# Last three down products in two PSUM banks, the last remainder on DVE, and the last output store in four

## The chip, the cores and the metric

The kernel runs on one core of one Trainium2 chip. The metric is the device time of one execution in microseconds (us); a lower number is better. The engines are PE (TensorE, matrix products, with PEld for its weight loads), DVE (VectorE), ACT (ScalarE), POOL (GpSimd) and SP (SyncE, which here only issues DMA transfers). PE writes into PSUM, which has eight banks of 128 x 512 fp32; DVE and ACT read PSUM, POOL doesn't.

## The reference

`x` is 4 sequences x 512 tokens x 128 features. Four residual layers follow each other: a gated state-space layer, a mixture of experts, a time-mixing layer (RWKV), and the same mixture of experts again. Only the last one's end is touched by the change. It is:

```python
x = hidden_states.reshape(-1, h)
scores = jax.nn.softmax(x @ gate_w, axis=-1)
topk_w, topk_idx = jax.lax.top_k(scores, K)
topk_w = topk_w / (jnp.sum(topk_w, axis=-1, keepdims=True) + 1e-20)
onehot = jax.nn.one_hot(topk_idx, E, dtype=x.dtype)
w_per_expert = jnp.einsum('nke,nk->ne', onehot, topk_w)
for e in range(E):
    hid = jax.nn.silu(x @ w_gate[e]) * (x @ w_up[e])
    y = y + w_per_expert[:, e:e + 1] * (hid @ w_down[e])
shared = jax.nn.silu(x @ ws_gate) * (x @ ws_up) @ ws_down
return (y + shared).reshape(b, s, h)
```

with 8 experts, 2 chosen for each token, and a hidden width of 256; its input is the layer-normed `x`, and its result is added to `x`. All is in fp32; the kernel splits each fp32 operand of these products into an fp16 high part and an fp16 remainder and makes three products of them.

## The kernel before

The last three layers run in one phase, `phase_body`. Each engine has its own stream of instructions, written out by hand; between engines only semaphores order the work (`wait_ge` and `then_inc`).

The experts' work is cut into 8 slots (`q`), four sequences for the first mixture and four for the second, and each slot into 9 branches (`e`; 0 is the shared one). A unit `u = 9 q + e` is one branch on one sequence of 512 tokens, and there are UNITS = 72. The time-mixing layer of each sequence is laid in between (`beside`), the last of it well before the last slot. In a unit:

- `gate_up(u, blk)` on PE makes the gate and the up product for each half `blk` of the hidden width, 3 matmuls each (L1571, L1572, L1575), in banks 0 to 3.
- `gate` on ACT (L1762) applies silu; `hidden` on DVE (L1925) multiplies by the up product into `hid`.
- `high` on ACT (L1769) casts `hid` to fp16, `hid_hi`; `low` on POOL (L2160) makes the remainder `hid_lo = hid - hid_hi` and increments `lo_ready`.
- `down(u)` on PE makes for each of the four 128-token tiles 6 matmuls (L1590 to L1592), 24 in all, into one bank, `down_ps` (bank 4), and increments `down_made`. It waits for `lo_ready` 2(u + 1) and for `added` u, since the add of the unit before reads the same bank.
- `add(u)` on DVE (L1941) adds the four tiles, each with its tokens' expert weights, from `down_ps` into `x`; the last of the four increments `added`.

PE's stream is gate_up(u), then down(u - 2); after gate_up(71) come down(69), down(70) and down(71) with nothing between. DVE's is add(u - 3), then the two `hidden` of u; at its end stand add(69), add(70) and add(71). POOL's ends with the three remainders (70, 1), (71, 0), (71, 1). Bank 5, `ps_t`, serves for turning (transposing) tiles and for parts of the time-mixing layer; its last use is the turn of slot 7's input, read by ACT, which then increments `normT_ready` to 7.

SP stores a sequence of the output when `added` says that its ninth branch is in: one transfer of 256 KB per sequence (L2315), 128 partitions x 4 tiles x 512 bytes. Its last instruction waits for all stores.

Of the kernel before, what the change touches and what calls it, by code (L numbers as in the profile page):

```python
# [13 lines left out]
P = 128  # L14
SEQS, SEQ = 4, 512
TPS = SEQ // P
# [11 lines left out]
FBLK = FFN // P  # L28
# [9 lines left out]
ALU = mybir.AluOpType  # L38
# [1391 lines left out]
def of_seq(s):  # L1430

    return slice(TPS * s, TPS * (s + 1))
# [9 lines left out]
def phase_body(core, io, lns, moe_x):  # L1442
# [4 lines left out]
    nc = core.nc  # L1447
    SLOTS = 2 * SEQS
    UNITS = SLOTS * BRANCHES
    HB = HIDDEN // P  # L1450
    with ExitStack() as ctx:
        def sb(name, shape, dt=F32):
            return ctx.enter_context(nc.sbuf_tensor("b_" + name, shape, dt))

        def sem(name):
            return core.semaphore("b_" + name)

        x, w = core.x, core.wsplit
# [7 lines left out]
        hid = sb("hid", [P, 4, SEQ])  # L1466
        hid_hi = sb("hid_hi", [P, 3 * FBLK, SEQ], F16)
        hid_lo = sb("hid_lo", [P, 3 * FBLK, SEQ], F16)
# [42 lines left out]
        gate_ps, up_ps, down_ps = core.banks[0:2], core.banks[2:4], core.banks[4]  # L1511
        ps_t, ps_k, ps_v = core.banks[5:8]

        def table(k):
# [5 lines left out]
        recip = ps_k  # L1522

        gate_made, up_made, down_made = core.gate_made, core.up_made, sem("down")
        silu_ready, hid_ready, hi_ready, lo_ready, added = sem("silu"), sem("hid"), sem("hid_hi"), sem("hid_lo"), sem("added")
        veps_in, rstd_in, normed, x_turned, normT_ready, x_hi_ready, x_lo_ready = (
            sem("veps_in"), sem("rstd_in"), sem("normed"), sem("x_turned"), sem("normT"), sem("x_hi"), sem("x_lo"))
# [17 lines left out]
        dve_step, pool_step, act_step, stored = sem("dve_step"), sem("pool_step"), sem("act_step"), sem("stored")  # L1545
# [14 lines left out]
        def _(pe):  # L1560
# [15 lines left out]

            def down(u):
                e = u % BRANCHES
                pe.wait_ge(lo_ready, 2 * (u + 1))
                if u:  # L1580
                    pe.wait_ge(added, u)
                for c in range(TPS):
                    dst = down_ps[:, P * c:P * (c + 1)]
                    for blk in range(FBLK):
                        slot = FBLK * (u % 3) + blk
                        h_hi = hid_hi[:, slot, P * c:P * (c + 1)]
                        h_lo = hid_lo[:, slot, P * c:P * (c + 1)]
                        d_hi = w[:, e, 4, P * blk:P * (blk + 1)]
                        d_lo = w[:, e, 5, P * blk:P * (blk + 1)]
                        nc.tensor.matmul(dst, h_hi, d_hi, start=blk == 0, stop=False)  # L1590
                        nc.tensor.matmul(dst, h_hi, d_lo, start=False, stop=False)  # L1591
                        ins = nc.tensor.matmul(dst, h_lo, d_hi, start=False, stop=blk == FBLK - 1)  # L1592
                ins.then_inc(down_made, 1)
# [151 lines left out]
            for u in range(UNITS + 2):  # L1745
                if u < UNITS:
                    if u:
                        gate_up(u, 0)
                    beside(u, 0)
                    if u:  # L1750
                        gate_up(u, 1)
                    beside(u, 1)
                if u >= 2:
                    down(u - 2)
                if u < UNITS:
                    beside(u, 2)
# [155 lines left out]
        def _(dve):  # L1912
# [7 lines left out]
            def hidden(u, blk):  # L1920
                dve.wait_ge(silu_ready, 2 * u + blk + 1)
                dve.wait_ge(up_made, 2 * u + blk + 1)
                if u >= 2:
                    dve.wait_ge(lo_ready, 2 * (u - 2) + blk + 1)
                nc.vector.scalar_tensor_tensor(hid[:, 2 * (u % 2) + blk, :], up_ps[blk][:, :], GU_UNSCALE * H_SCALE,  # L1925
                                               silu[:, 2 * (u % 2) + blk, :], ALU.mult, ALU.mult).then_inc(hid_ready, 1)

            def add(u):
                q, e = divmod(u, BRANCHES)
                s = q % SEQS  # L1930
                dve.wait_ge(down_made, u + 1)
                if e == 0:
                    nc.vector.scalar_tensor_tensor(x[:, of_seq(s), :], down_ps[:, :]
                                                   .rearrange("p (c d) -> p c d", c=TPS), DOWN_UNSCALE,
                                                   x[:, of_seq(s), :], ALU.mult, ALU.add).then_inc(added, 1)
                    return
                if e == 1:
                    dve.wait_ge(routed, q + 1)
                for c in range(TPS):
                    i = TPS * s + c  # L1940
                    ins = nc.vector.scalar_tensor_tensor(x[:, i, :], down_ps[:, P * c:P * (c + 1)],  # L1941
                                                         w_branch[:, q % 2, e, c:c + 1], x[:, i, :], ALU.mult, ALU.add)
                ins.then_inc(added, 1)

            def all_experts(ap):
# [190 lines left out]
                        aggregate(ln_m2, s, veps_in)  # L2136

            for u in range(UNITS + 3):
                if u >= 3:
                    add(u - 3)  # L2140
                if u < UNITS:
                    beside(u, 0)
                    hidden(u, 0)
                    beside(u, 1)
                    hidden(u, 1)
                    beside(u, 2)

        @block.gpsimd
        def _(pool):
# [7 lines left out]
            def low(u, blk):  # L2157
                pool.wait_ge(hi_ready, 2 * u + blk + 1)
                slot = FBLK * (u % 3) + blk
                nc.gpsimd.tensor_tensor(hid_lo[:, slot, :], hid[:, 2 * (u % 2) + blk, :], hid_hi[:, slot, :],  # L2160
                                        ALU.subtract).then_inc(lo_ready, 1)
# [136 lines left out]
            for u in range(UNITS):  # L2298
# [3 lines left out]
                beside(u, 1)  # L2302
                low(u, 0)
                beside(u, 2)
            low(UNITS - 1, 1)

        @block.sync
        def _(sp):
            core.clear_retired(sp)
            for dst, name in ((w_rkvo, "w_rkvo"), (w_fk, "w_fk"), (w_fr, "w_fr"), (w_fv, "w_fv")):  # L2310
                sp.dma_start(dst[:], io[name]).then_inc(w_b_in, 16)
            dst = io["out"].rearrange("s (c p) d -> s p c d", p=P)
            for s in range(SEQS):
                sp.wait_ge(added, (SEQS + s + 1) * BRANCHES)
                sp.dma_start(dst[s], x[:, of_seq(s), :]).then_inc(stored, 16)  # L2315
            sp.wait_ge(stored, 16 * SEQS)


class Shared:
# [3 lines left out]
def program(nc, io, stop_after=9):  # L2323
    core = Core(nc)
    with ExitStack() as top:
        constants(core, top)
        ln_moe1, ln_moe2, ln_tm, ln_cm = (LayerNorm(nc, top, name) for name in ("ln_moe1", "ln_moe2", "ln_tm", "ln_cm"))
        moe_x = (top.enter_context(nc.sbuf_tensor("normT_moe", [P, SEQ], F32)),
                 top.enter_context(nc.sbuf_tensor("x_hi", [P, 2, SEQ], F16)),
                 top.enter_context(nc.sbuf_tensor("x_lo", [P, 2, SEQ], F16)))  # L2330
        with ExitStack() as mamba:
            sh = Shared()
            sh.normT, sh.x_hi, sh.x_lo = moe_x

            def sb(name, shape, dt=F32):
                return mamba.enter_context(nc.sbuf_tensor(name, shape, dt))
            sh.ln = ln_moe1
            sh.norm = sb("norm", [P, TILES, P])
            sh.q = sb("q", [P, TILES, P])
            sh.xbc = sb("xbc", [P, CONV_BLOCKS, TOKENS])  # L2340
            sh.sz = sb("sz", [P, TILES, INNER])
            sh.xtok = sb("xtok", [P, TILES, XTOK])
            sh.moe_raw = sb("moe_raw", [P, MOE_RING, 3 * FFN])
            sh.w_out = sb("w_out", [P, 2, P])
            sh.w_out_in = top.enter_context(nc.semaphore("w_out_in"))
            phase_mamba(core, io, sh)
            core.end_phase()
        phase_body(core, io, (ln_moe1, ln_moe2, ln_tm, ln_cm), moe_x)
        core.end_phase()
        core.end_phase()  # L2350
# [63 lines left out]
```

## Time and profile before

| | |
|---|---|
| median of 3 runs | 497.91 us (497.86 to 498.1) |
| the profiled execution | 496.6 us |
| span of its trace, first to last instruction | 494.9 us |
| PE busy | 470.8 us (95%) |
| DVE busy | 389.5 us (79%) |
| ACT busy | 355.9 us (72%) |
| POOL busy | 366.7 us (74%) |
| first product of down(69) | 483.85 us |

The profile is of one execution. Busy time is what the engine's own instructions cover; issuing a DMA, waiting and branching aren't counted. A row in order of time gives the start, the duration, the engine, the line, the tile written and the tiles read, how many instructions were merged (x4), and in brackets how long the engine had been idle and which instruction released it. PE's matmuls are pipelined: a row of 0.22 us may start 0.06 us behind the one before. The span leaves out what lies around the program; the median of the runs is 1.3 us above the profiled execution.

### The profile page before, as it was taken

To read this page: it belongs to the slowest core of one execution; us is meant where nothing else is said; L and a number is where in the kernel's file an instruction comes from. 1 tells how busy PE (TensorE), PEld (TensorE's weight loads), DVE (VectorE), ACT (ScalarE), POOL (GpSimd) and SP (SyncE) were. 2 spreads that over 40 slices of the span, in tenths; PEclk is the share of its full clock that TensorE was granted. 3 is DMA by queue.
4 is the path that set the end of the run, shared out by engine and by line. 5 is a ranking of instruction groups with operands and counts; after the bars stand their busy time and mean duration, and the time that the engine had idled before them with its cause. 6 is when DMAs were issued, how large, how long until landed. Compare 5 with 4: busy or idle time off the path is not lost.

```text
span 494.9 us, 10643 instructions
## 1 busy us (share of the span) xinstructions
PE 470.8 (95%) x3706; PEld 325.5 (66%) x3706; DVE 389.5 (79%) x1043; ACT 355.9 (72%) x687; POOL 366.7 (74%) x449
## 2 busy tenths in 40 slices
PE   7898999999899999999999999999999989999994
PEld 7575789988466666656566756576566766766663
DVE  5899999677767878799888897889887868487663
ACT  1699999774857767964996759695868576858551
POOL 4755896986485775899878978987989585366652
PEclk9999999999999999999999999999999999999999
DMA  8000212000200000000000000000000000000000
GB/s 270 20 2 11 66 53 66 1 1 3 71 1 1 1 1 2 3 0 1 2 1 1 3 1 1 1 1 2 2 23 1 1 1 23 2 2 1 21 1 23
DMA packets 7013, 8.51 MB, mean 17 GB/s; under 512 B 560, under 2 KB 5168, under 8 KB 6960
## 3 DMA queue, kind: packets, MB, share of 16 engines
q1 hardware_dynamic: 6960, 7.83, 4.9%
q8 instruction: 30, 0.49, 0.4%
q14 instruction: 23, 0.19, 0.1%
HBM read 6.78 MB, written 1.05 MB: 16 GB/s over the span
## 4 chain that ended last, share of the span: by engine, by line
PE 55%; DVE 9%; POOL 5%; ACT 3%; issue 2%; DVEq 0%; POOLq 0%; ACTq 0%
PE bank L1571 9%; PE bank L1575 9%; PE bank L1572 9%; PE bank L1590 5%; PE bank L1592 5%; PE bank L1591 5%; PE bank L1707 3%; PE bank L1690 2%; PE bank L1633 2%; DVE x L1941 2%; PE bank L1634 2%; POOL b_hc L2222 1%; PE bank L1597 1%; DVE b_hid L1925 1%; PE bank L1618 1%
## 5 line engine op out<-in xcount | busy, mean ns | idle before, releaser
L2160 POOL TENSOR_TENSOR b_hid_lo<-b_hid,b_hid_hi 128x512 f16<-128x512 f32 x144 | 168.0, 1179 | 51.4 <-ACT b_hid_hi L1769 49.3
L1925 DVE SCALAR_TENSOR_TENSOR b_hid<-bank,b_silu 128x512 f32<-128x512 f32 x144 | 97.7, 688 | 55.4 <-ACT b_silu L1762 38.1
L1762 ACT ACTIVATE b_silu<-bank 128x512 f32<-128x512 f32 x144 | 85.9, 597 | 57.6 <-PE bank L1575 56.5
L1571 PE MATMUL bank<-x_hi,wsplit 128*128 128x512 f16 x284 | 107.7, 379 | 2.4 <-ACT b_silu L1762 1.9
L1575 PE MATMUL bank<-x_lo,wsplit 128*128 128x512 f16 x284 | 107.6, 379 | 0.0
L1572 PE MATMUL bank<-x_hi,wsplit 128*128 128x512 f16 x284 | 107.6, 379 | 0.0
L1590 PE MATMUL bank<-wsplit,b_hid_hi 128*128 128x128 f16 x576 | 100.2, 219 | 4.3 <-DVE x L1941 2.6
L1769 ACT CAST b_hid_hi<-b_hid 128x512 f16<-128x512 f32 x144 | 88.2, 612 | 22.2 <-DVE b_hid L1925 22.0
L1592 PE MATMUL bank<-wsplit,b_hid_lo 128*128 128x128 f16 x576 | 100.2, 219 | 0.0
L1591 PE MATMUL bank<-wsplit,b_hid_hi 128*128 128x128 f16 x576 | 100.2, 219 | 0.0
L1941 DVE SCALAR_TENSOR_TENSOR x<-bank,b_w_branch,x 128x128 f32<-128x128 f32 x256 | 71.5, 342 | 15.5 <-PE bank L1592 15.4
L1590 PEld LDWEIGHTS bank<-wsplit,b_hid_hi 128*128 128x128 f16 x576 | 56.6, 98 | 15.2 <-POOL b_hid_lo L2160 5.6
L1591 PEld LDWEIGHTS bank<-wsplit,b_hid_hi 128*128 128x128 f16 x576 | 56.3, 98 | 7.1 <-issue 1.3
L1592 PEld LDWEIGHTS bank<-wsplit,b_hid_lo 128*128 128x128 f16 x576 | 56.3, 98 | 0.0
L1575 PEld LDWEIGHTS bank<-x_lo,wsplit 128*128 128x128 f16 x284 | 27.8, 98 | 33.6
L1571 PEld LDWEIGHTS bank<-x_hi,wsplit 128*128 128x128 f16 x284 | 27.9, 98 | 29.7 <-issue 2.9
L1572 PEld LDWEIGHTS bank<-x_hi,wsplit 128*128 128x128 f16 x284 | 27.8, 98 | 26.7 <-issue 4.0
L520 DVE SCALAR_TENSOR_TENSOR xbc<-bank,cols,xbc 128x511 f32<-128x511 f32 (+2 forms) x48 | 35.6, 746 | 1.8 <-ACT xbc L783 0.7
L1114 PE MATMUL bank<-causal,seg_l 128*128 128x128 f32 x128 | 17.2, 278 | 0.4 <-ACT expo L828 0.2
L1145 PEld LDWEIGHTS bank<-xdt,mix 128*128 128x128 f32 x128 | 16.4, 192 | 0.7
L1114 PEld LDWEIGHTS bank<-causal,seg_l 128*128 128x128 f32 x128 | 15.9, 192 | 1.4 <-issue 0.9
L341 POOL TENSOR_TENSOR g<-y,sz 128x256 f32<-128x256 f32 x16 | 13.2, 825 | 4.5 <-DVE y L595 4.5
(246 smaller groups left out, 946.4 us busy)
## 6 DMA issues: line engine op xcount, KB each, us to landing
moe_raw<-in_moe SPq DMA_DIRECT2D x9, 384.0 KB, 4.1
x<-in_x SPq DMA_DIRECT2D x4, 256.0 KB, 3.9
out<-x SPq DMA_DIRECT2D x4, 256.0 KB, 2.3
rope<-in_rope SPq DMA_DIRECT2D x1, 512.0 KB, 6.2
wzx<-in_wzx SPq DMA_DIRECT2D x1, 386.0 KB, 6.5
b_w_rkvo<-in_w_rkvo SPq DMA_DIRECT2D x1, 256.0 KB, 2.7
b_w_fk<-in_w_fk SPq DMA_DIRECT2D x1, 256.0 KB, 2.9
b_w_fv<-in_w_fv SPq DMA_DIRECT2D x1, 256.0 KB, 3.4
```

The source lines that it names most:

```text
L520: ins = nc.vector.scalar_tensor_tensor(xbc[:, b, t0 + back:t1], conv_ps[b % 2][:, 0:SEQ - back], col(core, "conv_w", TAPS * b + TAPS - 1 - ...
L1571: nc.tensor.matmul(dst, hi, x_hi[:, q % 2, :], start=True, stop=False)
L1572: nc.tensor.matmul(dst, lo, x_hi[:, q % 2, :], start=False, stop=False)
L1575: nc.tensor.matmul(dst, hi, x_lo[:, q % 2, :], start=False, stop=True).then_inc(made, 1)
L1590: nc.tensor.matmul(dst, h_hi, d_hi, start=blk == 0, stop=False)
L1591: nc.tensor.matmul(dst, h_hi, d_lo, start=False, stop=False)
L1592: ins = nc.tensor.matmul(dst, h_lo, d_hi, start=False, stop=blk == FBLK - 1)
L1762: nc.scalar.activation(silu[:, 2 * (u % 2) + blk, :], gate_ps[blk][:, :], ACT.Silu, scale=GU_UNSCALE).then_inc(silu_ready, 1)
L1769: nc.scalar.copy(hid_hi[:, FBLK * (u % 3) + blk, :], hid[:, 2 * (u % 2) + blk, :]).then_inc(hi_ready, 1)
L1925: nc.vector.scalar_tensor_tensor(hid[:, 2 * (u % 2) + blk, :], up_ps[blk][:, :], GU_UNSCALE * H_SCALE, silu[:, 2 * (u % 2) + blk, :], ALU. ...
L1941: ins = nc.vector.scalar_tensor_tensor(x[:, i, :], down_ps[:, P * c:P * (c + 1)], w_branch[:, q % 2, e, c:c + 1], x[:, i, :], ALU.mult, AL ...
L2160: nc.gpsimd.tensor_tensor(hid_lo[:, slot, :], hid[:, 2 * (u % 2) + blk, :], hid_hi[:, slot, :], ALU.subtract).then_inc(lo_ready, 1)
```

## The change

Three edits, all at the end of the program. The down products of units 69 and 71 go to bank 5 and the one of 70 stays in bank 4; the waits follow, so that a down product waits for the reader of its own bank. The remainder (71, 1) is made by DVE (`last_low`, with a semaphore of its own), ahead of add(69) in DVE's stream, and no longer by POOL. The last sequence is stored in four transfers of 64 KB, one for each 128-token tile, each released by that tile's add.

```diff
+        def down_bank(u):
+
+            return ps_t if u in (UNITS - 3, UNITS - 1) else down_ps
...
+        last_lo = sem("last_lo")
...
             def down(u):
                 e = u % BRANCHES
-                pe.wait_ge(lo_ready, 2 * (u + 1))
-                if u:
+                if u == UNITS - 1:
+                    pe.wait_ge(lo_ready, 2 * UNITS - 1)
+                    pe.wait_ge(last_lo, 1)
+                else:
+                    pe.wait_ge(lo_ready, 2 * (u + 1))
+                if u == UNITS - 3:
+                    pe.wait_ge(normT_ready, SLOTS - 1)
+                if u > UNITS - 3:
+                    pe.wait_ge(added, u - 1)
+                elif u and u < UNITS - 3:
                     pe.wait_ge(added, u)
                 for c in range(TPS):
-                    dst = down_ps[:, P * c:P * (c + 1)]
+                    dst = down_bank(u)[:, P * c:P * (c + 1)]
...
+            def last_low():
+
+                u = UNITS - 1
+                slot = FBLK * (u % 3) + FBLK - 1
+                dve.wait_ge(hi_ready, 2 * UNITS)
+                nc.vector.tensor_tensor(hid_lo[:, slot, :], hid[:, 2 * (u % 2) + FBLK - 1, :], hid_hi[:, slot, :],
+                                        ALU.subtract).then_inc(last_lo, 1)
+
             def add(u):
...
                 dve.wait_ge(down_made, u + 1)
+                if u > UNITS - 3:
+                    dve.wait_ge(added, u)
...
                 for c in range(TPS):
                     i = TPS * s + c
-                    ins = nc.vector.scalar_tensor_tensor(x[:, i, :], down_ps[:, P * c:P * (c + 1)],
+                    ins = nc.vector.scalar_tensor_tensor(x[:, i, :], down_bank(u)[:, P * c:P * (c + 1)],
                                                          w_branch[:, q % 2, e, c:c + 1], x[:, i, :], ALU.mult, ALU.add)
+                    if u == UNITS - 1 and c < TPS - 1:
+                        ins.then_inc(added, 1)
                 ins.then_inc(added, 1)
...
             for u in range(UNITS + 3):
+                if u == UNITS:
+                    last_low()
                 if u >= 3:
                     add(u - 3)
...
-            low(UNITS - 1, 1)
...
-            for s in range(SEQS):
+            for s in range(SEQS - 1):
                 sp.wait_ge(added, (SEQS + s + 1) * BRANCHES)
                 sp.dma_start(dst[s], x[:, of_seq(s), :]).then_inc(stored, 16)
-            sp.wait_ge(stored, 16 * SEQS)
+            for c in range(TPS):
+                sp.wait_ge(added, UNITS + c)
+                sp.dma_start(dst[SEQS - 1][:, c, :], x[:, TPS * (SEQS - 1) + c, :]).then_inc(stored, 16)
+            sp.wait_ge(stored, 16 * (SEQS - 1 + TPS))
```

The end of DVE's stream before, from the `hidden` pair of unit 71 on; the rows of L1941 are the adds of units 68 to 71, and the square brackets name what a row waits for:

```order
L1941 SCALAR_TENSOR_TENSOR x<-bank4,b_w_branch,x 128x128 x3
L1925 SCALAR_TENSOR_TENSOR b_hid<-bank2,b_silu 128x512 [waits b_hid_lo,up_made,b_silu]
L1925 SCALAR_TENSOR_TENSOR b_hid<-bank3,b_silu 128x512 [waits b_hid_lo,up_made,b_silu]
L1941 SCALAR_TENSOR_TENSOR x<-bank4,b_w_branch,x 128x128 [waits b_down]
L1941 SCALAR_TENSOR_TENSOR x<-bank4,b_w_branch,x 128x128 x3
L1941 SCALAR_TENSOR_TENSOR x<-bank4,b_w_branch,x 128x128 [waits b_down]
L1941 SCALAR_TENSOR_TENSOR x<-bank4,b_w_branch,x 128x128 x3
```

The same place now (L1939 is `hidden`, L1965 the add):

```order
L1965 SCALAR_TENSOR_TENSOR x<-bank4,b_w_branch,x 128x128 x3
L1939 SCALAR_TENSOR_TENSOR b_hid<-bank2,b_silu 128x512 [waits b_hid_lo,up_made,b_silu]
L1939 SCALAR_TENSOR_TENSOR b_hid<-bank3,b_silu 128x512 [waits b_hid_lo,up_made,b_silu]
L1947 TENSOR_TENSOR b_hid_lo<-b_hid,b_hid_hi 128x512 [waits b_hid_hi]
L1965 SCALAR_TENSOR_TENSOR x<-bank5,b_w_branch,x 128x128 [waits b_down]
L1965 SCALAR_TENSOR_TENSOR x<-bank5,b_w_branch,x 128x128 x3
L1965 SCALAR_TENSOR_TENSOR x<-bank4,b_w_branch,x 128x128 [waits b_added,b_down]
L1965 SCALAR_TENSOR_TENSOR x<-bank4,b_w_branch,x 128x128 x3
```

The remainder has moved in ahead of add(69), add(69) and add(71) read bank 5, and add(70) and add(71) wait for `added` as well. The last add of each list, like the one above it, is left out.

The end of SP's stream before, from the weight loads at the phase's start on:

```order
L2311 DMA b_w_rkvo<-in_w_rkvo 128x512
L2311 DMA b_w_fk<-in_w_fk 128x512
L2311 DMA b_w_fr<-in_w_fr 128x128
L2311 DMA b_w_fv<-in_w_fv 128x512
L2315 DMA out<-x 128x4x128 [waits b_added] x4
L1451 UNCONDITIONAL_BRANCH [waits b_stored]
```

And now:

```order
L2338 DMA b_w_rkvo<-in_w_rkvo 128x512
L2338 DMA b_w_fk<-in_w_fk 128x512
L2338 DMA b_w_fr<-in_w_fr 128x128
L2338 DMA b_w_fv<-in_w_fv 128x512
L2342 DMA out<-x 128x4x128 [waits b_added] x3
L2345 DMA out<-x 128x128 [waits b_added] x4
L1451 UNCONDITIONAL_BRANCH [waits b_stored]
```

One store of four tiles has become four stores of one tile.

## Rows read from the trace of the kernel before

**Rows 1.** The page, engines: busy us, share of the span, instructions

```profile
PE 470.8 (95%) x3706; PEld 325.5 (66%) x3706; DVE 389.5 (79%) x1043; ACT 355.9 (72%) x687; POOL 366.7 (74%) x449
```

**Rows 2.** DVE in order of time, the tail (start us, duration us)

```profile
481.46 1.12 DVE L1941 SCALAR_TENSOR_TENSOR x<-bank,b_w_branch,x 128x128 f32<-128x128 f32 x4 [0.58 <-PE bank L1592]
482.82 0.69 DVE L1925 SCALAR_TENSOR_TENSOR b_hid<-bank,b_silu 128x512 f32<-128x512 f32 x1 [0.23 <-ACT b_silu L1762]
...
485.39 1.13 DVE L1941 SCALAR_TENSOR_TENSOR x<-bank,b_w_branch,x 128x128 f32<-128x128 f32 x4 [0.58 <-PE bank L1592]
488.21 1.13 DVE L1941 SCALAR_TENSOR_TENSOR x<-bank,b_w_branch,x 128x128 f32<-128x128 f32 x4 [1.69 <-PE bank L1592]
491.02 1.13 DVE L1941 SCALAR_TENSOR_TENSOR x<-bank,b_w_branch,x 128x128 f32<-128x128 f32 x4 [1.68 <-PE bank L1592]
```

**Rows 3.** PE in order of time: down(69)'s last product, first of 70 and 71

```profile
485.14 0.22 PE L1592 MATMUL bank<-wsplit,b_hid_lo 128*128 128x128 f16 x1
486.67 0.22 PE L1590 MATMUL bank<-wsplit,b_hid_hi 128*128 128x128 f16 x1 [1.31 <-DVE x L1941]
...
489.48 0.22 PE L1590 MATMUL bank<-wsplit,b_hid_hi 128*128 128x128 f16 x1 [1.31 <-DVE x L1941]
```

**Rows 4.** Chain that ended last, 480 to 496 us (start, us, what)

```profile
490.99 0.03 issue
491.02 0.35 DVE x L1941
```

**Rows 5.** ACT and POOL in order of time, the tail

```profile
482.11 0.60 ACT L1762 ACTIVATE b_silu<-bank 128x512 f32<-128x512 f32 x1 [1.53 <-PE bank L1575]
...
484.90 0.62 ACT L1769 CAST b_hid_hi<-b_hid 128x512 f16<-128x512 f32 x1 [0.39 <-DVE b_hid L1925]
484.59 2.27 POOL L2160 TENSOR_TENSOR b_hid_lo<-b_hid,b_hid_hi 128x512 f16<-128x512 f32 x2
```

**Rows 6.** DVE groups: busy us, mean ns | idle before; L2071: min/median/max ns

```profile
L626 DVE TENSOR_TENSOR x_lo<-normT_moe,x_hi 128x512 f16<-128x512 f32 x1 | 0.7, 684 | 0.0
L1962 DVE TENSOR_TENSOR b_shift<-bank,b_best 128x32 f32<-128x32 f32 x8 | 1.5, 192 | 0.3
L2071 DVE SCALAR_TENSOR_TENSOR b_mixed<-b_dif,cols,b_hcT x8: 741/1698/1753, 259.6 to 416.7; 128x512 f32<-128x512 f32 x8
```

**Rows 7.** DVE and POOL in order of time, around 112 us

```profile
112.20 0.68 DVE L626 TENSOR_TENSOR x_lo<-normT_moe,x_hi 128x512 f16<-128x512 f32 x1
111.69 0.62 POOL L314 TENSOR_TENSOR dx<-xtok,cols 128x256 f32<-128x256 f32 x1
```

**Rows 8.** SP's DMA issues in order of time (start us, us on SP)

```profile
6.64 2.13 SPq L245 DMA_DIRECT2D moe_raw<-in_moe  x3
...
130.26 0.33 SPq L2311 DMA_DIRECT2D b_w_rkvo<-in_w_rkvo  x1
130.64 0.51 SPq L2311 DMA_DIRECT2D b_w_fk<-in_w_fk  x1
131.20 0.42 SPq L2311 DMA_DIRECT2D b_w_fr<-in_w_fr  x1
131.67 0.43 SPq L2311 DMA_DIRECT2D b_w_fv<-in_w_fv  x1
...
492.17 0.37 SPq L2315 DMA_DIRECT2D out<-x  x1
```

**Rows 9.** DMA: us to landing; tenths busy, 129:137; stages: engines' busy, clock, share, GB/s

```profile
out<-x SPq DMA_DIRECT2D x4, 256.0 KB, 2.3
b_w_fr<-in_w_fr SPq DMA_DIRECT2D x1, 64.0 KB, 3.0
...
DMA  0000000100044979979978778435000000000000
...
493.00:493.10 0.10, 0.00 (x0) 0.00 (x0) 0.00 (x0) 0.00 (x0) 0.00 (x0) 1.00 0.09 26
494.00:494.10 0.10, 0.00 (x0) 0.00 (x0) 0.00 (x0) 0.00 (x0) 0.00 (x0) 1.00 0.26 67
```

More of the change, by code:

```diff
@@ L1931, in add @@
                 dve.wait_ge(down_made, u + 1)
+                if u > UNITS - 3:
+                    dve.wait_ge(added, u)
                 if e == 0:
-                    nc.vector.scalar_tensor_tensor(x[:, of_seq(s), :], down_ps[:, :]
+                    nc.vector.scalar_tensor_tensor(x[:, of_seq(s), :], down_bank(u)[:, :]
                                                    .rearrange("p (c d) -> p c d", c=TPS), DOWN_UNSCALE,
```

## The prediction

> **What bounds the kernel now.** Read first the engines' shares, then the last 11 us of DVE and PE in order of time with what released each, then the chain in the same stretch. Over the whole span PE is busy 95% [rows 1]; the change leaves everything up to unit 69 alone, so only the tail is of interest. There the picture differs from the rest: DVE's last two adds stood idle 1.69 and 1.68 us for PE [rows 2], and PE's first products of units 70 and 71 stood idle 1.31 us each for DVE's add [rows 3]. Each waits for the other, because the down product of a unit and its add share one bank. In the order of time [rows 2, 3]: down(69) issues its last product at 485.14, add(69) runs 485.39 to 486.52, down(70) runs from 486.67, add(70) 488.21 to 489.34, down(71) from 489.48, add(71) 491.02 to 492.15. So a round is 2.81 us: 1.13 of add, about 0.15 to release PE, 1.51 of 24 products, 0.03 to release DVE [rows 2 to 4]. Steady units don't show this: there gate and up products of a later unit stand between two down products. After add(71) comes the store: SP issues at 492.17, data moves from about 493.05 to 494.05, the store has landed 2.3 us after its issue, at 494.47, and the span ends at 494.9, another 0.43 [rows 8, 9]. The profiled execution took 496.6 us for a span of 494.9; the median of the runs is 497.91, 1.3 above. All that changes is in a tail that both contain once, so I subtract microseconds from either alike.
>
> **Two banks.** down(69) goes to bank 5, whose last reader (normT_ready 7, the scaling of slot 7's turned input) stands seven units earlier in the code, so that wait costs nothing; it starts where it starts now, since its predecessor's add, done at 482.58 [rows 2], didn't hold it. down(70) uses bank 4 and needs only added 69, met at 482.58, and the remainder of (70, 1), which POOL had made before it began the next at 484.59 [rows 5]. It follows directly: the 24 products of a unit stand 0.056 apart (from 486.67 the last ends 1.51 later, itself 0.22 long [rows 3, 4]), so it starts at 485.20, its 24 take 1.35 to issue, its end is about 486.72 instead of 488.18. The first of the two stalls of 1.31 is gone. down(71) goes to bank 5 and must wait for add(69), which reads it. With nothing else changed add(69) ends at 486.52, and PE's turn would be at 486.72; next late would be POOL's remainder of (71, 1), whose last two operations end at 484.59 + 2.27 = 486.86 [rows 5]. So what remains of the second stall is set by the third edit.
>
> **The last remainder on DVE.** It replaces a POOL operation (half of those 2.27, ending at 486.86) by a DVE TENSOR_TENSOR of the same form, 128x512 f32 to f16, two SBUF inputs. The trace of before has exactly one such on DVE, L626, 0.684 us [rows 6]. It waits for ACT's last cast, 484.90 + 0.62 = 485.52, plus the 0.11 that DVE took after an ACT activation (482.11 + 0.60 to 482.82) [rows 2, 5]: it starts at 485.63 and ends at 486.31. But it stands ahead of add(69) on DVE, and add(69) could have started at 485.39. The queued work behind it is add(69), (70) and (71), and PE's down(71) waits for the first. add(69) becomes 486.32 to 487.45. That delays its end by 0.93, while the remainder itself is done 0.55 earlier than on POOL: on this path the move costs more than it gives, against the other two edits alone (PE at about 486.95). down(71): 487.45 + 0.15 = 487.60, + 1.51 = 489.11, + 0.03: add(71) starts at **489.14 instead of 491.02, 1.88 us earlier**. add(70), with its new wait for added 70, takes 487.50 to 488.63 (a wait between dependent DVE operations is 0.04: L1962, 0.3 us idle in 8 [rows 6]), half a microsecond before add(71) is released: hidden. The lower bound of the DVE start is 0.08 less, since DVE operations without a wait between them overlap by that much (the first of the four adds takes 0.35, all four 1.13 [rows 2, 4]).
>
> Is DVE slowed by sharing memory access with POOL? DVE's L2071, also with two SBUF inputs, takes 741 ns at best and 1698 at the median [rows 6]; the long ones may be ones that meet POOL. The POOL operation on (71, 0), the first of those 2.27 us, ends at about 485.73, 0.1 us after DVE's would start. L626 gives the case that fits: it began at 112.20 under a POOL operation that ran until 112.31, and took 0.684 [rows 6, 7]. I add nothing, and keep up to 0.96 (1698 - 741) as a rival. The Trainium skill, GPSIMD Engine Reference, in its table of properties, says that POOL's memory interface is shared with VectorE and contends with instructions that have two SBUF inputs. By that alone the operation could be the slow kind and 1.88 would shrink to about 0.9; the row of L626 says that an overlap this short is free.
>
> **Four transfers.** Before, from the start of add(71) to the end: 1.13 + 0.02, then 2.3, then 0.43, in all 3.88. Now tile 0 is released after its own 0.35 [rows 4], SP starts at 489.14 + 0.35 + 0.02 = 489.51. Tiles 1 to 3 are ready at 0.26 us each, but SP issues more slowly: the four weight loads start at 130.26, 130.64, 131.20 and 131.67, a pitch of 0.47; they range from 0.38 to 0.56 [rows 8]. So the last issue is at 489.51 + 3 x 0.47 = 490.92, which is 0.63 later than a single transfer's (490.29). SP's issue takes the place of DVE as the last wait. What a lone store of 64 KB needs the trace doesn't show. Built from the 256 KB store: 0.88 until data moves, 1.0 of data, 0.42 until landed [rows 9]; a quarter of the data is 0.25, so 1.55. Bounds: 1.55 and the full 2.3. I take 1.55, for the four weight loads, last issued at 131.67, moved data without a pause from the 12th to the 28th fifth of a microsecond behind 129, thus from 131.2 to 134.6 [rows 9], so neighbours overlap. End: 490.92 + 1.55 + 0.43 = 492.90; from the start of add(71) that is 3.76 against 3.88, a gain of 0.12 only. The sum is **1.88 + 0.12 = 2.00 us**: span 492.9, median 497.91 - 2.00 = **495.9**. The same pieces with a pitch of 0.38 give 2.27, with 0.56 give 1.73; with 0.71, the pitch of the three L245 that stood behind nine queued transfers [rows 8], 1.28. The DVE overlap can add 0.08 to each.
>
> The Trainium skill, DMA: Bandwidth & Descriptors, section "Anatomy of one DMA — SWDGE (gpsimd) path", puts a DMA at about 2.0 us fixed plus bytes over 436 GB/s and says that most of the fixed part is the write receipt: it speaks against splitting. Estimated from that page, 64 KB would need 2.15 where I count 1.55, and the total gain would be 1.4; for the 256 KB store it gives 2.6 where this trace has 2.3. It is weighed as the first rival.
>
> **Rivals.** (1) Landing doesn't shrink with size: a 64 KB store needs the same 2.3 as 256 KB. Then the tail after add(71) is 0.37 + 1.41 + 2.3 + 0.43 = 4.51, 0.63 worse than before, and the gain is 1.25: 496.7. For it: the 64 KB weight load took 3.0 [rows 9]. Against it: that one was queued behind 512 KB, and the store's own rows show a microsecond of data in the 2.3. The page named above would come near this. (2) DVE's remainder is held by POOL and costs 0.96 more: gain 1.0, 496.9. It needs POOL's (71, 0) to hold DVE's whole operation for an overlap of 0.1. (3) Slower: the queue works the four stores off one after another, each to its receipt. Each then holds it for 1.55: 489.51 + 4 x 1.55 + 0.43 = 496.14, 1.2 over 494.9: 499.1. The kernel is slower from 1.24 us a store on. Against it stands the row of the four loads, which carried data without a gap. (4) The change does not do what it says, because DVE is now the wait: add(69) still stands before down(71). That I have counted in; it is why the gain is 1.9 and not the 2.6 of both stalls. A larger gain, 2.35 and more, needs a quick SP and a landing below 1.55.
>
> **How the numbers follow.** Forecast, 495.6 to 496.3: 64%. (1) 496.7: 15%. (2) 496.9: 9%, two thirds of it within 0.2% of before. (3) 499.1: 4%. Larger gain, below 495.6: 8%. The likeliest is 495.9. From 495.4 to 496.8 the range leaves out (3), most of (2) and the outer end of the larger gain, with (1) and what lies between taken in: near 2 in 10 with what I can't foresee. 0.2%, about what a measurement can tell from no change, is 1.0 us: faster is below 496.9, thus 64 + 15 + 8 + 3 = 90%, same 6%, slower 4%.
>
> **What would show it.** Right: PE's first product of down(70) stands 0.06 behind the last of down(69), with no idle; one PE stall of about 0.9 us is left, ahead of down(71), released by DVE's add; DVE shows the remainder of about 0.68 before add(69), and add(69) starts near 486.3; add(71) starts 1.9 earlier; four SP issues at a pitch near 0.47, the last 0.6 after DVE's last add; landing of each about 1.5. Wrong: a DVE remainder of 1.2 or more (2), landings of 2.3 (1), landings that grow from first to fourth by over a microsecond each (3), or any shift before 483.85, which nothing here accounts for.

## The result, and the profile after

| | before | after |
|---|---|---|
| median | 497.28 us (16 runs, 495.71 to 498.10) | 495.05 us (16 runs, 494.49 to 496.12) |
| profiled execution, its span | 496.6, 494.9 us | 494.99, 493.3 us |
| down(69)'s first product to the span's end ("tail") | 11.05 us | 8.95 us |

The ratio is 0.9959 with a 95% interval of 0.995 to 0.9969: faster by 2.0 us (1.5 to 2.5). The forecast gain was 2.00. The absolute time, 495.05, lies below the low end of 495.4. More runs of the kernel before stood beside these; over all 16 its median is 497.28, not the 497.91 of the three runs that the prediction started from. A span is given to 0.1 us, so a tail is known to about 0.05.

DVE's tail after, in order of time, which answers to [rows 2]:

```profile
484.61 0.69 DVE L1939 SCALAR_TENSOR_TENSOR b_hid<-bank,b_silu 128x512 f32<-128x512 f32 x1 [0.60 <-PE bank L1581]
486.04 0.75 DVE L1947 TENSOR_TENSOR b_hid_lo<-b_hid,b_hid_hi 128x512 f16<-128x512 f32 x1 [0.74 <-ACT b_hid_hi L1783]
486.71 2.34 DVE L1965 SCALAR_TENSOR_TENSOR x<-bank,b_w_branch,x 128x128 f32<-128x128 f32 x8
489.51 1.13 DVE L1965 SCALAR_TENSOR_TENSOR x<-bank,b_w_branch,x 128x128 f32<-128x128 f32 x4 [0.46 <-PE bank L1606]
```

PE's, which answers to [rows 3]: the first product of unit 69, the two rows around the border between 69 and 70 (485.63, 485.69), and the last of 70 and the first of 71:

```profile
484.35 0.22 PE L1604 MATMUL bank<-wsplit,b_hid_hi 128*128 128x128 f16 x1
...
485.63 0.22 PE L1606 MATMUL bank<-wsplit,b_hid_lo 128*128 128x128 f16 x1
485.69 0.22 PE L1604 MATMUL bank<-wsplit,b_hid_hi 128*128 128x128 f16 x1
...
486.97 0.22 PE L1606 MATMUL bank<-wsplit,b_hid_lo 128*128 128x128 f16 x1
487.98 0.22 PE L1604 MATMUL bank<-wsplit,b_hid_hi 128*128 128x128 f16 x1 [0.79 <-DVE x L1965]
```

Both stalls of 1.31 us are no more; one of 0.79 is left, and DVE's add releases it. ACT's last cast runs 485.39 to 486.01, so DVE's remainder begins 0.03 behind it. SP's stores, and their time to landing, which answer to [rows 8, 9]:

```profile
489.89 1.77 SPq L2345 DMA_DIRECT2D out<-x  x4
```

```profile
out<-x SPq DMA_DIRECT2D x4, 64.0 KB, 1.6
```

Four issues take 1.77 us; DVE has been done since 490.64 when the last one begins at about 491.23.

Everything below is counted from the first product of down(69), so that what happens earlier drops out.

| from down(69)'s first product, us | before | forecast | after |
|---|---|---|---|
| DVE's remainder starts | none | 1.78 | 1.69 |
| add(69) starts | 1.54 | 2.47 | 2.36 |
| down(71) starts | 5.63 | 3.75 | 3.63 |
| add(71) starts | 7.17 | 5.29 | 5.16 |
| span ends | 11.05 | 9.05 | 8.95 |

### The profile page after: what moved, and what is told of

It reads as the page before. It is cut to its first block, busy times and chain, and to the rows that moved or that the text cites. A ratio compares the mean times of both kernels' runs of the same rounds, so it can differ in the third digit from the quotient of the medians.

```text
span 493.3 us, 10648 instructions
## 1 busy us (share of the span) xinstructions
PE 471.2 (96%) x3706; PEld 326.2 (66%) x3706; DVE 390.1 (79%) x1044; ACT 355.8 (72%) x687; POOL 365.6 (74%) x448
## 4 chain that ended last, share of the span: by engine, by line
PE 54%; DVE 9%; POOL 5%; ACT 4%; issue 2%; DVEq 0%; ACTq 0%; POOLq 0%
PE bank L1577 9%; PE bank L1581 9%; PE bank L1578 9%; PE bank L1604 5%; PE bank L1606 5%; PE bank L1605 5%; PE bank L1721 3%; PE bank L1704 2%; PE bank L1647 2%; PE bank L1648 2%; POOL b_hc L2250 1%; DVE x L1965 1%; DVE b_hid L1939 1%; PE bank L1611 1%; PE bank L1632 1%
## 5 line engine op out<-in xcount | busy, mean ns | idle before, releaser
L1939 DVE SCALAR_TENSOR_TENSOR b_hid<-bank,b_silu 128x512 f32<-128x512 f32 x144 | 97.7, 688 | 55.4 <-ACT b_silu L1776 38.1
L1965 DVE SCALAR_TENSOR_TENSOR x<-bank,b_w_branch,x 128x128 f32<-128x128 f32 x256 | 71.5, 341 | 12.1 <-PE bank L1606 11.9
```

What stands on the lines that cost most here:

```text
L1965: ins = nc.vector.scalar_tensor_tensor(x[:, i, :], down_bank(u)[:, P * c:P * (c + 1)], w_branch[:, q % 2, e, c:c + 1], x[:, i, :], ALU.mul ...
```

## The experiments

### Which edit carries what

Three kernels take one or two of the edits, from the changed kernel. Two banks alone:

```diff
             def down(u):
-                if u == UNITS - 1:
-                    pe.wait_ge(lo_ready, 2 * UNITS - 1)
-                    pe.wait_ge(last_lo, 1)
-                else:
-                    pe.wait_ge(lo_ready, 2 * (u + 1))
+                pe.wait_ge(lo_ready, 2 * (u + 1))
...
-                if u == UNITS:
-                    last_low()
...
+            low(UNITS - 1, 1)
```

and one store of the last sequence as in the kernel before. Where the remainder isn't ahead of it, add(69) also waits for `added` 69, which has long been reached.

> Two banks alone; the last remainder on POOL as before and one store of 256 KB. Theory A: from the first product of down(69), add(69) starts at 1.54 us, down(71) waits for POOL's last remainder (3.01, plus some 0.1) and add(71) starts at 4.64 instead of 7.17 before and 5.16 in the changed kernel; the tail is 8.5 us against 11.05 and 8.95; some 2.5 us faster than before. Rival B (moving the remainder to DVE is what lets the banks pay): add(71) starts at 5.2 or later and the tail is 9.0 or more.

> Two banks and four stores, the last remainder on POOL: the changed kernel without its edit on DVE. Theory A: tail 8.4 us, 0.5 shorter than the changed kernel's 8.95, some 2.6 us faster than before. Rival B: tail 8.95 or more.

> Two banks and the remainder on DVE, one store of 256 KB: the changed kernel without its four stores. Theory A: add(71) starts 5.16 after the first product of down(69) as in the changed kernel, 3.88 follow, tail 9.04: 2.0 us faster than before and 0.1 slower than the changed kernel. Rival (four stores carry a good part of the gain): tail 9.4 or more.

Measured, from the profiles:

| kernel | add(69) | down(71) | add(71) | add(71) to end | tail | ratio to before (95%) |
|---|---|---|---|---|---|---|
| before | 1.54 | 5.63 | 7.17 | 3.88 | 11.05 | 1 |
| all three edits | 2.36 | 3.63 | 5.16 | 3.79 | 8.95 | 0.9959 (0.995 to 0.9969) |
| banks | 1.54 | 3.06 | 4.61 | 3.86 | 8.47 | 0.9951 (0.9935 to 0.9966) |
| banks, four stores | 1.54 | 3.06 | 4.61 | 3.76 | 8.37 | 0.9945 (0.9928 to 0.9961) |
| banks, remainder on DVE | 2.36 | 3.62 | 5.15 | 3.82 | 8.97 | 0.9955 (0.9937 to 0.9974) |

Banks with four stores, PE and then POOL in order of time:

```profile
486.89 0.23 PE L1600 MATMUL bank<-wsplit,b_hid_hi 128*128 128x128 f16 x1 [0.22 <-POOL b_hid_lo L2182]
```

```profile
483.26 3.57 POOL L2182 TENSOR_TENSOR b_hid_lo<-b_hid,b_hid_hi 128x512 f16<-128x512 f32 x3 [1.48 <-ACT b_hid_hi L1779]
```

POOL ends at 486.83 and PE stands idle only 0.22. Each tail came out within 0.1 us of what theory A gave: the banks bring 2.6, the four stores 0.1 at most (8.47 to 8.37 with POOL's remainder, 8.97 to 8.95 with DVE's), and making the remainder on DVE takes back 0.5 to 0.6. The ratios of the three variants lie within 0.001 of each other and their intervals overlap, so this ranking rests on the profiles, whose tails carry little of the scatter described below: the kernel before, profiled twice, has 11.05 and 11.00.

The two smaller edits alone, on one bank:

> The kernel before with only the last remainder moved to DVE, ahead of add(69); one bank, one store. Theory A: add(69) starts 2.36 us after the first product of down(69) instead of 1.54, everything behind it shifts by this, tail 11.05 + 0.82 = 11.87: 0.8 us slower than before. Rival: the move costs nothing, because PE's down(71) no longer waits for POOL: tail 11.05 or less.

> The kernel before with only its last store split in four. Theory A: from the start of add(71) to the end 3.79 us instead of 3.88, tail 10.95; no difference that a median can tell. Rival (the landing of a small store is what counts): landings of 64 KB take 2.3, tail 11.7.

```profile
487.14 1.11 DVE L1961 SCALAR_TENSOR_TENSOR x<-bank,b_w_branch,x 128x128 f32<-128x128 f32 x4
489.93 1.13 DVE L1961 SCALAR_TENSOR_TENSOR x<-bank,b_w_branch,x 128x128 f32<-128x128 f32 x4 [1.68 <-PE bank L1602]
492.75 1.13 DVE L1961 SCALAR_TENSOR_TENSOR x<-bank,b_w_branch,x 128x128 f32<-128x128 f32 x4 [1.68 <-PE bank L1602]
```

These are the three adds with only the remainder moved (first product of down(69) at 484.78): add(69) starts at 2.36, the round of 2.8 us stays, the tail is 11.82, and the kernel is slower: 498.50 us, ratio 1.0027 (1.0015 to 1.0039). Without the banks the edit on DVE is a loss by itself. The tail shows 0.77 of it, near the 0.8 expected; the 1.3 of the ratio is more than the edit costs, because all ten runs of this kernel have the drop of the clock described below, and nine of the 19 runs beside them. Against those nine (median 498.06) it is 0.44 slower. Only the last store split: tail 10.93, ratio 0.9998 (0.9986 to 1.0011), no difference. Both tails are as theory A had them.

### Where the remainder stands, and whether POOL holds DVE

> The changed kernel with DVE's remainder behind add(69) instead of ahead of it. Theory A: add(69) at 1.54 to 2.67 from the first product of down(69), the remainder until 3.35, down(71) released by it at 3.5, add(71) at 5.0, tail 8.8, 0.15 shorter than the changed kernel. Rival (the order on DVE makes no difference): tail 8.95.

```diff
-                if u == UNITS:
-                    last_low()
                 if u >= 3:
                     add(u - 3)
+                if u == UNITS:
+                    last_low()
```

Its add(69) waits for `added` 69 too. Tail 8.66 against 8.95, better than the 8.8 expected: DVE starts the remainder at 2.58, before add(69) ends at 2.67, it takes 0.68, and PE starts down(71) at 3.36, released by it. So the order within DVE matters, 0.3 us here. The ratio is 0.9934 (0.991 to 0.996); with four runs it can't be told from the changed kernel's.

> The changed kernel, and POOL makes the last remainder a second time, into a tile that nobody reads, released by the same cast as DVE's. So both engines run an operation with two SBUF inputs side by side. If POOL holds DVE (the second rival of the prediction, made to happen): DVE's remainder takes 1.4 to 1.8 us instead of 0.75 and the tail grows from 8.95 by as much. If the two only share and lose little: 0.75 to 0.85, tail 9.0.

```diff
+            pool.wait_ge(hi_ready, 2 * UNITS)
+            nc.gpsimd.tensor_tensor(lo_twice[:], hid[:, 2 * ((UNITS - 1) % 2) + FBLK - 1, :], hid_hi[:, slot, :],
+                                    ALU.subtract)
```

DVE, then POOL:

```profile
484.52 0.75 DVE L1948 TENSOR_TENSOR b_hid_lo<-b_hid,b_hid_hi 128x512 f16<-128x512 f32 x1 [0.74 <-ACT b_hid_hi L1784]
```

```profile
484.68 1.60 POOL L2336 TENSOR_TENSOR b_lo_twice<-b_hid,b_hid_hi 128x512 f16<-128x512 f32 x1
```

DVE's operation has POOL's beside it for all but its first 0.16 us and takes the same 0.75; POOL's takes 1.60 instead of 1.16 (the median of its 143 others). The tail is 8.88. Here DVE began first, and POOL was the one that lost. It is one pair in one profile.

The other order stands in the trace before, at the long L2071 [rows 6] that the prediction's second rival was priced from. DVE and POOL:

```profile
259.60 1.70 DVE L2071 SCALAR_TENSOR_TENSOR b_mixed<-b_dif,cols,b_hcT 128x512 f32<-128x512 f32 x1
415.27 2.13 DVE L2071 SCALAR_TENSOR_TENSOR b_mixed<-b_dif,cols,b_hcT 128x512 f32<-128x512 f32 x2
```

```profile
259.58 1.17 POOL L2160 TENSOR_TENSOR b_hid_lo<-b_hid,b_hid_hi 128x512 f16<-128x512 f32 x1
413.80 2.39 POOL L2160 TENSOR_TENSOR b_hid_lo<-b_hid,b_hid_hi 128x512 f16<-128x512 f32 x2
```

At 259.60 POOL began 0.02 ahead, kept its 1.17, and DVE took 1.70. The last two L2071 start at 415.27 and 416.67; POOL is done at 416.19, and the first takes 1.47, the second, with POOL idle, 0.74. The six of 1.69 to 1.75 all stand beside POOL operations with two inputs. So the rival's mechanism exists, at the price of up to 0.96 that it was given, where POOL began first and the two overlapped for long. In the changed kernel POOL also began first, but the overlap was 0.20 us (POOL until 486.24, DVE from 486.04), and the remainder took 0.75; in the kernel with the remainder behind add(69), with POOL done, it took 0.68, so at most 0.07 went to it. No run starts a long overlap in POOL's favour on purpose.

### The stores

> Two banks, the last remainder on POOL, and the last sequence stored in two transfers of 128 KB (tiles 0 and 1, tiles 2 and 3) instead of four. Theory A (SP's pitch of some 0.47 us bounds four stores, 0.6 us behind DVE's last add): with two, the last issue follows DVE's last add at once, 1.15 after the start of add(71); landing 0.88 + 0.5 + 0.42 = 1.8; with the last 0.43, 3.4 us from the start of add(71) instead of 3.76 to 3.79 with four and 3.88 with one; tail 8.0 against 8.37. Rival (what counts is the size of the last transfer): tail 8.4 or more.

```diff
-            for c in range(TPS):
-                sp.wait_ge(added, UNITS + c)
+            for a, b in [(0, 2), (2, 4)]:
+                sp.wait_ge(added, UNITS + b - 1)
```

DVE's last adds, SP's issues, and the issues with KB and us to landing:

```profile
489.48 1.13 DVE L1961 SCALAR_TENSOR_TENSOR x<-bank,b_w_branch,x 128x128 f32<-128x128 f32 x4 [0.61 <-PE bank L1602]
```

```profile
490.12 0.89 SPq L2340 DMA_DIRECT2D out<-x  x2
```

```profile
out<-x SPq DMA_DIRECT2D x2, 128.0 KB, 1.8
```

From the start of add(71) to the end 3.42 us, forecast 3.4; with four stores 3.76 to 3.79, with one 3.82 to 3.88. Two stores gain what four give away to SP's pitch. This too rests on the profiles: the ratio, 0.9932 (0.9916 to 0.9949), overlaps the 0.9945 (0.9928 to 0.9961) of two banks with four stores. The stores land 2.3, 1.8 and 1.6 us after issue for 256, 128 and 64 KB.

### Why the absolute time missed

The kernel before, unchanged, under another label:

> The kernel before, unchanged. Theory A (the gain was right and the absolute time missed only because three runs of the kernel before stood at the upper end of its scatter): its median is within 0.2% of the kernel before that runs beside it, its runs scatter over about 2 us, and where they differ, the difference is there before the first router product of the last phase, not in the tail. Rival B (the changed kernel gained more than the tail holds, through something earlier): the kernel before scatters by less than 1 us, and its tail, 11.05 us from the first product of down(69) to the span's end, differs from run to run.

Its median is 496.81 us (11 runs, 496.38 to 498.05), ratio 0.9997 (0.9987 to 1.0007). The scatter of 1.7 us is there with nothing changed, and its profiled tail is 11.00, as before. Where the scatter is made shows in the start-up loop: PE multiplies an identity 22 times (44 matmuls, L1183) while the first tokens are normalised. Its row before, with two banks alone, and with banks and remainder on DVE:

```profile
2.27 7.42 PE L1183 MATMUL bank<-ident 128*128 128x128 f32 x44 [2.27 <-POOL after L265]
```

```profile
2.27 8.06 PE L1183 MATMUL bank<-ident 128*128 128x128 f32 x44 [2.27 <-POOL after L265]
```

```profile
2.26 6.54 PE L1183 MATMUL bank<-ident 128*128 128x128 f32 x44 [2.26 <-POOL after L265]
```

The same loop takes 6.54 to 8.06 us in the profiles, and the first router product of the last phase starts at 126.2, 126.9 and 125.3: in all twelve profiles with this loop the start is the loop's duration plus 118.7 to 118.9. The changed kernel's profile has 7.92 and 126.8, the one before 7.42 and 126.2, which is the 0.5 us by which its down(69) starts later (484.35, 483.85). In the loop a matmul takes about 0.18 us at first and 0.09 later, and the switch comes between 3 and 6 us behind the loop's start. By stages of 2 us (the first bracket counts PE's matmuls), banks and remainder on DVE:

```profile
4.00:6.00 2.00, 2.00 (x15) 2.00 (x15) 1.13 (x9) 0.00 (x0) 0.73 (x1) 1.00 0.91 263
6.00:8.00 2.00, 2.00 (x21) 2.00 (x20) 1.93 (x12) 0.00 (x0) 1.14 (x4) 1.00 1.02 321
```

and two banks alone:

```profile
4.00:6.00 2.00, 2.00 (x11) 2.00 (x11) 1.03 (x8) 0.00 (x0) 0.82 (x1) 1.00 0.92 269
6.00:8.00 2.00, 2.00 (x12) 2.00 (x11) 1.85 (x12) 0.00 (x0) 0.95 (x4) 1.00 0.99 320
```

Between 6 and 8 us the one makes 21 and the other 12. The granted clock reads 1.00 (2.4 GHz) in all of these rows, so what makes them slow isn't seen in it.

There is a second source. In four profiles (remainder alone, split alone, two stores, tile banks) PE's granted clock drops between 130 and 140 us. Remainder alone, by stage:

```profile
125.00:130.00 5.00, 3.90 (x22) 1.99 (x20) 3.25 (x13) 4.10 (x7) 1.95 (x16) 1.00 0.01 2
130.00:135.00 5.00, 3.85 (x11) 1.39 (x12) 3.56 (x13) 4.04 (x8) 3.32 (x3) 0.71 0.53 174
135.00:140.00 5.00, 5.00 (x47) 3.16 (x46) 2.31 (x4) 2.71 (x6) 4.32 (x9) 0.95 0.00 0
```

Behind the engines' columns stands the granted clock: 0.71 of 2.4 GHz as a mean over five microseconds, a mixture of the levels 2.4 and 1.2 GHz; by single microseconds it reads 0.56, 0.50, 0.50 and 0.73 from 132 to 136. PE had been busy 3.90 of the 5 us ahead of it; in the kernel before, profiled without a drop, it was 4.54, but the kernel with 16 start-up products (below) had 3.63 and no drop, so what sets it off stays open. From the first router product to down(69) these four take 359.2 to 359.3 us, the ten profiles without a drop 357.4 to 357.6. The loop with 1.5 us and the drop with 1.7 cover the range of 2.4 us that the kernel before has.

Whether a run had the drop can be read without its profile, from the mean granted clock of the whole run: it is 0.995 or 0.997 for these four and 0.998 or more for the other ten. It is on record for 54 more runs of the kernel before, the 11 above and 43 beside the experiments:

| mean granted clock | before: runs, us, median | changed kernel: runs, us, median |
|---|---|---|
| 0.999 to 1.000 | 31, 495.56 to 497.27, 496.75 | 12, 494.49 to 495.15, 494.89 |
| 0.995 to 0.997 | 23, 497.37 to 498.18, 497.86 | 4, 495.48 to 496.12, 495.83 |

The two groups don't overlap. The three runs of the prediction, 497.86 to 498.10, lie where only runs with a drop lie (their own clocks aren't on record), and the profiled execution, 496.6 with a clock of 1.000, in the other group. Like against like the change gains 1.9 and 2.0 us by these medians, though the runs didn't stand side by side.

> The changed kernel with 16 instead of 22 products in the start-up loop that keeps PE busy until the first tokens are normalised. Ten profiles say that the first router product of the last phase starts 118.8 us after that loop's duration, which varies from 6.54 to 8.06 us. Theory A (the scatter of absolute times, and so the base of the prediction, comes from this loop, which ends later than its tokens): the loop takes 5.9 us or less, the first router product starts at 125.0 or earlier, and the median falls by some 0.8 us below the changed kernel's 495.05. Rival (PE's clock is what rises late, and the products behind the loop only run slow in its place): the start stays between 125.3 and 126.9.

```diff
-            warm_up(22)
+            warm_up(16)
```

Its PE in order of time:

```profile
2.27 5.89 PE L1183 MATMUL bank<-ident 128*128 128x128 f32 x32 [2.27 <-POOL after L265]
7.99 1.08 PE L1018 MATMUL bank<-ident,norm 128*128 128x128 f32 x4
```

The loop takes 5.89 as expected and the first router product starts at 125.2, not 125.0 or before. The first four real products take 1.08 us where they take 0.60 in the kernel before, but the slow stretch didn't move into them: PE makes 12 matmuls between 7 and 8 us, as many as anywhere in the loop. They wait for the tokens. DVE normalises the first four tiles here, 0.26 us apart and the last until 8.69, and PE's four products start 0.25 apart, the last at 8.74. DVE's row here, and in the kernel before:

```profile
7.58 1.11 DVE L494 TENSOR_SCALAR norm<-x,rstd,nbias 128x128 f32<-128x128 f32 x4
```

```profile
6.96 1.11 DVE L494 TENSOR_SCALAR norm<-x,rstd,nbias 128x128 f32<-128x128 f32 x4
```

There the four tiles are done at 8.07, and PE turns to them only at 9.53. So with 16 products DVE bounds the start, and a shorter loop would have little left to gain. Median 493.21 us, ratio 0.9915 (0.99 to 0.993) against 0.9959 with the full loop: faster by more than the 0.8 us expected. None of its four runs has the drop (clock 0.999 and 1.000). They are 1.7 us below the 494.89 that the changed kernel has without a drop, and the profiled first router product is 1.6 earlier (125.2, 126.8), so most of the gain is the start. Profiles with the full loop get there too when their loop is short: banks with DVE's remainder 493.44, and the run with POOL's second remainder 493.46.

### A faster version

Down(71) tile by tile in banks 0 to 3, whose gate and up products have been read by then, with a count per tile; remainder on POOL; stores issued by SP and ACT by turns:

```diff
+        def down_tile(u, c):
+            if u == UNITS - 1:
+                return (gate_ps + up_ps)[c][:, 0:P]
+            return down_bank(u)[:, P * c:P * (c + 1)]
...
+                    if u == UNITS - 1 and c < TPS - 1:
+                        ins.then_inc(down_made, 1)
...
+                    if u == UNITS - 1 and c:
+                        dve.wait_ge(down_made, u + 1 + c)
...
+            for a, b in [(1, 2), (3, 4)]:
+                act.wait_ge(added, UNITS + b - 1)
+                nc.scalar.dma_start(dst[SEQS - 1][:, a:b, :],
+                                    x[:, TPS * (SEQS - 1) + a:TPS * (SEQS - 1) + b, :]).then_inc(stored, 16)
```

> Built on the readings: remainder on POOL, down(69), (70) in banks 4 and 5, and down(71) tile by tile in banks 0 to 3 with a count for each tile, so that an add follows its tile's six products; four stores, issued by SP and ACT by turns. Theory A: DVE's adds of unit 71 begin behind add(70), at some 4.05 us from the first product of down(69), the last ends at 5.1 instead of 5.74; last issue 5.15, landing 1.55, end 7.1: 1.2 to 1.3 us shorter than two banks and four stores (8.37), 3.9 shorter than before. Rival (ACT's DMA issue or the waits per tile eat it): tail 8 or more.

> Both together, the fastest version that the readings suggest: tile banks, stores from two queues, POOL's remainder and 16 start-up products. Theory A: the two gains add, tail 7.1, start at 125.0 or earlier, some 4.5 to 5 us below the kernel before. Rival as for 16 products alone: only the tail's 3.9.

The first of the two in order of time, DVE, ACT's queue and SP's queue:

```profile
487.68 2.35 DVE L1976 SCALAR_TENSOR_TENSOR x<-bank,b_w_branch,x 128x128 f32<-128x128 f32 x8 [0.21 <-PE bank L1608]
```

```profile
489.55 0.88 ACTq L1931 DMA_DIRECT2D out<-x  x2
```

```profile
489.29 0.86 SPq L2355 DMA_DIRECT2D out<-x  x2
```

Eight tile adds now follow each other, with no wait for PE between units 70 and 71. The tail is 7.20 us (7.1 expected, 3.85 below before); 493.37 us, ratio 0.9914 (0.9892 to 0.9935). With 16 start-up products the tail is 7.28; 492.11 us, ratio 0.9892 (0.9873 to 0.9911): 5.4 us faster than before and the fastest of all. Part of that is luck with the drop, which one of its four runs has and four of the seven beside it; by the medians of the runs without one it is 5.1, against the 4.5 to 5 expected. Its profiled loop took 6.67 for 32 matmuls and its router product started at 125.5, so the start wasn't the 125.0 expected.

## Why the prediction was right or wrong, point by point

- **Two banks: right.** down(70) follows down(69) at once and one stall is left, released by DVE's add. The stall is 0.79, forecast 0.9.
- **The remainder on DVE: right, and the costly one.** It was put at 0.684 behind a release of 0.11; it took 0.75 behind 0.03, and add(69) began 0.08 before it ended. The chain down to add(71) gained 2.01 us, forecast 1.88; of the 0.13 the shorter release gives 0.08 and the overlap, which the prediction named and left out of its sum, another 0.08, and the longer remainder takes back 0.07. The release had been read off a DVE operation that waits for PE's up product too, which may have been the later of the two. That the edit loses against POOL was said in the prediction ("the move costs more than it gives"), with 0.65 between the PE starts (486.95, 487.60); measured 0.57.
- **Four stores: right.** From add(71) to the end 3.79, forecast 3.76. The pitch was 0.45, forecast 0.47; the landing 1.5 to 1.6, forecast 1.55. The gain from it is 0.02 to 0.12 in the three pairs of profiles that differ only by it (8.97 and 8.95, 8.47 and 8.37, 11.05 and 10.93), forecast 0.12; the 0.05 to which a tail is known makes no more of it.
- **Rivals.** Landing that doesn't shrink (1) fell: 2.3, 1.8, 1.6 us. The Trainium skill, DMA: Bandwidth & Descriptors, section "Anatomy of one DMA — SWDGE (gpsimd) path", gives its 2.0 us and 436 GB/s for DMAs issued from GpSimd. These stores are issued by SP, so the prediction applied it to a path that it isn't stated for; its sum for 64 KB, 2.15, is 0.55 over what they took. POOL holding DVE (2) didn't occur in the changed kernel, where the remainder took 0.75 and not 1.2 or more, nor where the overlap was made on purpose. The reason is the short overlap: the long L2071 are DVE operations that POOL did hold. The prediction's "an overlap this short is free" came out at 0.07 or less. The Trainium skill, GPSIMD Engine Reference, in its table of properties, names the contention, and the traces agree: on POOL's side 1.60 for 1.16, on DVE's 1.70 for 0.74. One store after another (3) fell with the landings.
- **The time: wrong, by its base.** The step that failed is "so I subtract microseconds from either alike", with 497.91 as the base. The three runs, 497.86 to 498.10, were at the upper edge of a scatter of 2.4 us, and they agreed so well that they looked like the kernel's time. They lie among the runs with a drop of the clock, which 23 of 54 other runs of the kernel before had and 4 of 16 of the changed one. The profiled execution, 1.3 lower, had none, and was a sign of the scatter; the range had no term for it. Against the changed kernel's four runs with a drop the forecast 495.9 holds (median 495.83); the median of all 16 is that of a kernel mostly without. From 497.28 the same 2.00 gives 495.28, 0.2 above the measured 495.05. The gain by medians is 2.23, by the ratio 2.0, by the profiled tails 2.10. That the ratio gives the forecast 2.00 so exactly is luck: its interval is 1.5 to 2.5, and the errors in the chain partly cancel.

## What to carry to other kernels

At the end of a program the steady rhythm is gone, and producer and reader of one bank alternate; a second bank for the last units removes that for nothing, but look at once for what then stands last, and leave work on an otherwise idle engine rather than put it ahead of the chain on the busy one. A store split in as many pieces as there are tiles pays only as long as the issuing queue keeps up: with a pitch of 0.45 us against tiles every 0.26, two pieces beat four by 0.34 us in the profiled tails. When three runs agree within 0.05% and the profiled execution stands 0.3% off, look at the granted clock of each, forecast a ratio, and widen the absolute range by that distance.

## What the runs showed of the hardware beyond that

- A loop of 44 identical fp32 matmuls at the start took 6.54 to 8.06 us in twelve profiles, with the granted clock reading 1.00, and all later work shifted with it.
- The granted clock can drop for some microseconds at a phase border where PE is less busy, at a cost of 1.7 us; the same code had 23 runs with it and 31 without. What sets it off stays open: one kernel had it in all ten runs, though it differs from the one before only in the tail.
- Side by side, with two SBUF inputs each, the one that began second lost: POOL's subtraction of 128x512 rose from 1.16 to 1.60 us beside a DVE subtraction that began 0.16 ahead and kept its 0.75; a DVE operation rose from 0.74 to 1.70 beside a POOL subtraction that began 0.02 ahead and kept its 1.17.
- ACT's and SP's queues issue stores equally fast, two in 0.88 and 0.86 us, and their 64 KB stores land alike, in 1.6 us.
